# Cross attention's last unit: all score steps ahead of most value products, and four value products between the first turns of the probabilities

## Chip, core and metric

The kernel runs on one core of a Trainium2 chip. The metric is the device time of one execution in microseconds (us), lower is better. A core has a matrix engine (PE, with its weight loads, PEld), a vector engine (DVE), a scalar engine (ACT), GpSimd (POOL) and SyncE (SP), which here only starts DMA transfers. Each engine runs its own instructions strictly in the order in which they are written and waits at semaphores for the others, so an instruction that waits holds up everything behind it on its engine.

## The reference

Three blocks follow one another on x of 8 x 64 tokens of width 512, all in float32: cross attention over a context of 8 x 1601 tokens, a differential attention between the heads of each token with a feed forward, and a mixture of 32 experts (6 per token). The change touches the end of the first:

```
def cross_attention(x_q, x_k, x_v):            # x_k = x_v = context, B=8, L=64, S=1601
    Q = (x_q @ W_Q + b_Q)  -> (B, 16 heads, L, 32)
    K = (x_k @ W_K + b_K)  -> (B, 16, S, 32)
    V = (x_v @ W_V + b_V)  -> (B, 16, S, 32)
    attn = softmax(Q @ K^T / sqrt(32))
    return (attn @ V) @ W_O + b_O
x = x + cross_attention(layernorm(x), ctx, ctx)
x = x + differential_attention_and_ffn(layernorm(x))   # per token: 32 x 32 products of heads, softmax, then att2 @ v
x = x + mixture_of_experts(layernorm(x))
```

## The kernel before

**Units.** `queries_and_cross_attention` runs 16 units (b, h): a batch b of 8 and a half h of the heads (8 heads, 256 columns of K and V). In each unit PE makes the values of its half for the 1601 context tokens as seven value products (`values(b, h, v)`, v = 0 to 6, two tiles of 128 tokens each, the last one tile of 65 rows; 24 matmuls, the last 12), and eight score steps (`scores(b, h, i)`, two groups g of heads by four chunks n of 402 tokens). Value product v goes to a bank of PSUM, the matrix engine's result memory, given by `V_BANK`; ACT casts it to the high part (L596) and DVE subtracts that to get the low part (L741). A score step fills two banks of 0 to 3 and DVE copies both to `prob`, taking the row maxima on the way (L754). When a group's four steps are kept, ACT takes its exponentials in place (`exponentials`, two of each group, L602).

**Turns.** Then come 14 turns (g, t), numbered n = 7g + t: `turn` transposes two tiles of the probabilities into bank 6 or 7 (L471), ACT casts them to the high part (L615), DVE forms the low part (L771), and `weigh` multiplies them with the values (L484) one turn later. After the seven turns of a group DVE adds the halves (L779), PE selects (L494), DVE scales and writes `oT` (`output`, L791). In every unit but the last the key products of the next unit (`keys`) stand between the turns; the last unit, (7, 1), has no next one, so nothing stands there.

**The order in the last unit before.** PE: v0, steps 0 and 1, v1, select, v2, steps 2 and 3, v3, v4, steps 4 and 5, v5, steps 6 and 7, v6, then the turns (`STEPS_BEHIND`). ACT: the casts of v0 to v6, with the exponentials of the second block's heads (`head_exponentials`, L656) behind v2 and the unit's own two behind v3 and v4. DVE follows the same order and carries in its gaps the work of one tile (128 tokens, number t = 2) of the second block: row maximum behind v0 (L845), its subtraction behind v1 (L852), `row_sum` behind v3 (L857 to L861), and the eight sums `reduce` 16 to 23 (L831), of which 16 and 17 stood behind v5 and v6 and the others behind turns 1, 2, 4, 6, 8 and 9.

**POOL.** It waits for `row_sum`, makes three small weights (L319 to L324), then eight products `attended(t, i)` (L334) into two buffers in turn: product i waits until DVE has summed product i - 2, and DVE's `reduce` 16 + i waits for product i. Behind the eighth sum POOL squares (L340), DVE takes the mean square (L865), ACT the root (L629), DVE the reciprocal (L872), POOL scales (L344).

**SP.** Behind the last value product (`v_full`) it loads rows, x, two tiles' data and the weight slabs 1 and 2 over the memory of the context and its weights, which are free then; behind the eighth sum (`red_done`, since POOL's two buffers are slab 0's memory, `x_tok`) it loads slab 0 (W_O) and six others. All engines meet at the end of the block; the second block (`last_head_and_feed_forward`) begins with POOL's bias on `oT` (L1158) and PE's product of `oT` with slab 0 (L1483).

Of the kernel before, what the change touches and what calls it, by code (L numbers as in the profile page):

```python
# [21 lines left out]
B, L, D = 8, 64, 512  # L22
# [13 lines left out]
NV = -(-ST // 2)  # L36
# [34 lines left out]
def queries_and_cross_attention(nc, a, keep):  # L71
# [6 lines left out]
    with ExitStack() as ctx:  # L78
# [106 lines left out]
        freed_by = (2, 4, 5, NV)  # L185

        @block.sync
        def _(sp):
# [91 lines left out]
            for s in (1, 2):  # L280
                sp.dma_start(keep["slabs"][s], a["slabs"][s]).then_inc(keep["w_loaded"][s], 16)
            sp.wait_ge(red_done, 24 * (TT - 1))
            for s in (0, 4, 3, 5, 6, 7, 8):
                place = slab[:].rearrange("p (k n) -> p k n", k=KD) if s == 0 else keep["slabs"][s]
                sp.dma_start(place, a["slabs"][s]).then_inc(keep["w_loaded"][s], 16)
# [95 lines left out]
        def _(pe):  # L381
# [20 lines left out]
            def values(b, h, v):  # L402

                if (b, h, v) == (0, 0, 0):
                    pe.wait_ge(wkv_lo_done, 2)
                    pe.wait_ge(q_lo_done, KD)
                if v < 2:
                    pe.wait_ge(pT_lo_done, b * 28 + (14 * h + 13 + v))
                elif v < 5:
                    pe.wait_ge(v_lo_done, b * 14 + (7 * h + v - 1))  # L410
                else:
                    pe.wait_ge(o_done, b * 4 + (2 * h + v - 4))
                f = slice(D + 256 * h, D + 256 * h + 256)
                for st in tiles(v):
                    r = rows(st)
                    for k in range(KD):
                        s = slice(P * st, P * st + r)
                        ins = mm3(nc, ps[0:r, V_BANK[v], 256 * (st % 2):256 * (st % 2) + 256], c_hi[:, k, s],
                                  c_lo[:, k, s], wkv_hi[:, k, f], wkv_lo[:, k, f], k == 0, k == KD - 1)
                ins.then_inc(v_full, 1)  # L420
# [38 lines left out]
            def turn(b, h, g, t):  # L459
                n = 7 * g + t  # L460
                if n < 2:
                    pe.wait_ge(v_lo_done, b * 14 + (7 * h + 5 - n))
                else:
                    pe.wait_ge(pT_lo_done, b * 28 + (14 * h + 14 + n - 1))
# [9 lines left out]
            def weigh(b, h, g, t):  # L474
                n = 7 * g + t
                pe.wait_ge(pT_lo_done, b * 28 + (14 * h + 14 + n + 1))
                if t == 0:
                    pe.wait_ge(v_lo_done, b * 14 + (7 * h + 6 + g))
# [45 lines left out]
            def unit(b, h, last):  # L524
# [3 lines left out]
                for v in range(NV):  # L528
                    values(b, h, v)
                    for i in STEPS_BEHIND[v]:  # L530
                        scores(b, h, i)
                    if v == 1 and (b or h):
                        select(*((b, 0) if h else (b - 1, 1)), 1)
                for g in range(2):
                    for t in range(NV):
                        turn(b, h, g, t)
                        if t == 2:
                            sums(b, h, g)
# [47 lines left out]
        def _(act):  # L586
# [6 lines left out]
            def values(b, h, v):  # L593
# [3 lines left out]
                               ps[0:r, V_BANK[v], 0:256 * w].rearrange("p (a c) -> p a c", c=64)).then_inc(v_hi_done, 1)  # L597
# [60 lines left out]
            def unit(b, h, last):  # L658
# [7 lines left out]
                for v in range(NV):  # L666
# [8 lines left out]
                for g in range(2):  # L675
                    for t in range(NV):
                        turned(b, h, g, t)
                        if (g, t) in ((0, 1), (0, 3)):
                            exponentials(b, h, 2 + t // 2)
# [51 lines left out]
        def _(dve):  # L731
# [6 lines left out]
            def values(b, h, v):  # L738
# [3 lines left out]
                                        ps[0:r, V_BANK[v], 0:256 * w].rearrange("p (a c) -> p a c", c=64),  # L742
# [131 lines left out]
            def behind_values(b, h, v):  # L874
# [17 lines left out]
                if b == B - 1 and v > 4:  # L892
                    reduce(t, 11 + v)

            def behind_turn(b, h, g, s):
# [24 lines left out]
                else:  # L920
                    if n in (1, 2, 4, 6, 8, 9):
                        reduce(t, 18 + (1, 2, 4, 6, 8, 9).index(n))
# [17 lines left out]
            def unit(b, h, last):  # L940
# [5 lines left out]
                for v in range(NV):  # L946
# [11 lines left out]
                for g in range(2):  # L958
                    for t in range(NV):
                        turned(b, h, g, t)  # L960
                        for half in () if last else HALVES_AT[7 * g + t]:
# [1317 lines left out]
```

## Time and profile before

| | |
|---|---|
| three runs | 1458.3, 1454.91, 1457.27 us, median 1457.27 |
| profiled execution | 1456.9 us, its span 1455.0 us (1.9 us lie outside the span) |
| granted PE clock, mean of the span | 0.988 |
| busy over the span | PE 96%, PEld 82%, DVE 64%, ACT 43%, POOL 42% |
| the last unit on PE | from 934.2 to 986 us; DVE's last output of it ends at 987.3 us |
| its value and score part | to 959.2 us, PE busy throughout |
| its 14 turns | 959.2 to 987.3 us, PE with gaps |

Times of the trace are us from the span's start. In a timeline a row gives start, duration, engine, line of the kernel, operation, output <- input, shapes and count; where the engine was idle before, how long and who released it stands in brackets. Matmuls are pipelined: how long PE is occupied is read from start to start.

### The profile page before, as it was taken

What the parts mean: (1) busy time and instruction counts of PE and PEld (TensorE: products, weight loads), DVE (VectorE), ACT (ScalarE), POOL (GpSimd) and SP (SyncE); (2) the same over time, 40 slices, a digit from 0 to 9 for tenths busy, and PEclk for the clock granted to TensorE, in tenths of its full rate; (3) what the DMA queues carried; (4) which work ended last, traced back from release to release, by engine and by line L of the source; (5) the groups of instructions that cost most, each with busy time, mean ns of one, the idle gap of its engine ahead of it and who ended that gap; (6) DMA issues with size and microseconds to landing.
All of it is one profiled execution on the core that took longest, in us unless ns stands there. A gap on an engine that the chain in (4) does not pass through costs nothing. (4 is left out here: it accounts for less than half of the span.)

```text
span 1455.0 us, 23749 instructions
## 1 busy us (share of the span) xinstructions
PE 1404.1 (96%) x8920; PEld 1191.6 (82%) x8920; DVE 926.0 (64%) x1991; ACT 624.5 (43%) x1065; POOL 607.5 (42%) x276
## 2 busy tenths in 40 slices
PE   6999999999999999999999999988899999999998
PEld 5999999999899998999998989973677646766664
DVE  6545555554388664459675547884942277988885
ACT  4345354354443534535335443452222124666663
POOL 5007007004464920737570246455840025566662
PEclk9999999999999999999999999999999899999999
DMA  5103004013001112300301310037000468999997
GB/s 208 70 2 95 1 5 132 1 41 122 32 5 46 57 33 73 118 7 5 103 2 69 105 56 2 1 136 306 1 1 1 155 242 298 364 365 371 366 370 212
DMA packets 62052, 166.50 MB, mean 114 GB/s; under 512 B 14851, under 2 KB 31747, under 8 KB 52870
## 3 DMA queue, kind: packets, MB, share of 16 engines
q1 hardware_dynamic: 52550, 143.17, 26.7%
q0 software_dynamic: 9408, 22.03, 6.1%
q8 instruction: 65, 1.06, 0.3%
q14 instruction: 29, 0.24, 0.1%
HBM read 145.77 MB, written 19.40 MB: 114 GB/s over the span
## 5 line engine op out<-in xcount | busy, mean ns | idle before, releaser
L66 PE MATMUL ps_x<-wkv_hi,c_hi 128*128 128x256 f32 (+1 forms) x832 | 241.2, 290 | 0.0
L68 PE MATMUL ps_x<-wkv_hi,c_lo 128*128 128x256 f32 (+1 forms) x832 | 234.2, 281 | 0.0
L67 PE MATMUL ps_x<-wkv_lo,c_hi 128*128 128x256 f32 (+1 forms) x832 | 234.2, 281 | 0.0
L293 POOL TENSOR_TENSOR c_hi<-c_raw,ones 128x1608 fp32r<-128x1608 f32 x30 | 88.2, 2940 | 323.5 <-DMA c_raw<-ctxT 323.5
L771 DVE TENSOR_TENSOR pT<-ps_x,pT 128x512 fp32r<-128x512 f32 (+1 forms) x224 | 145.1, 648 | 118.0 <-ACT pT L615 115.3
L66 PE MATMUL ps_x<-c_hi,wkv_hi 128*128 128x402 f32 x512 | 195.9, 383 | 13.7 <-DVE c_lo L977 12.4
L615 ACT CAST pT<-ps_x 128x512 fp32r<-128x512 f32 (+1 forms) x224 | 124.5, 556 | 160.7 <-PE ps_x L471 157.6
L596 ACT CAST vv<-ps_x 128x512 fp32r<-128x512 f32 (+1 forms) x112 | 62.1, 555 | 278.4 <-PE ps_x L68 278.4
L67 PE MATMUL ps_x<-c_lo,wkv_hi 128*128 128x402 f32 x512 | 178.0, 348 | 0.0
L68 PE MATMUL ps_x<-c_hi,wkv_lo 128*128 128x402 f32 x512 | 178.0, 348 | 0.0
L66 PEld LDWEIGHTS ps_x<-wkv_hi,c_hi 128*128 128x128 f32 (+1 forms) x832 | 153.5, 184 | 17.0 <-issue 17.0
L741 DVE TENSOR_TENSOR vv<-ps_x,vv 128x512 fp32r<-128x512 f32 (+1 forms) x112 | 72.9, 651 | 139.1 <-ACT vv L596 139.1
L312 POOL TENSOR_TENSOR x_tok<-t_q,t_k 128x1024 f32<-128x1024 f32 x48 | 114.2, 2398 | 98.7 <-PE ps_x L521 56.6
L68 PEld LDWEIGHTS ps_x<-wkv_hi,c_lo 128*128 128x128 f32 (+1 forms) x832 | 153.6, 185 | 0.0
L67 PEld LDWEIGHTS ps_x<-wkv_lo,c_hi 128*128 128x128 f32 (+1 forms) x832 | 153.2, 184 | 0.0
L484 PE MATMUL ps_x<-pT,vv 128*128 128x256 f32 (+1 forms) x832 | 138.7, 288 | 9.3 <-DVE pT L771 9.0
L735 DVE SCALAR_TENSOR_TENSOR kT_lo<-ps_x,bk,kT_hi 128x402 fp32r<-128x402 f32 x128 | 81.1, 634 | 94.1 <-ACT kT_hi L590 93.7
L484 PEld LDWEIGHTS ps_x<-pT,vv 128*128 128x128 f32 (+1 forms) x832 | 125.4, 189 | 15.4 <-DVE pT L771 13.7
L754 DVE TENSOR_SCALAR_CACHE_REDUCE prob<-ps_x 128x402 f32<-128x402 f32 (+1 forms) x256 | 131.1, 569 | 0.0
L471 PE MATMUL ps_x<-ident,prob 128*128 128x128 f32 (+1 forms) x832 | 127.7, 273 | 0.0
L296 POOL TENSOR_TENSOR c_lo<-c_raw,c_hi 128x1608 fp32r<-128x1608 f32 x31 | 113.4, 3659 | 19.0 <-ACT c_hi L709 16.6
L1722 POOL DMA_INDIRECT acc<-e_mix,e_row_out x40 | 90.1, 2254 | 69.1 <-ACT e_mix L1993 27.1
(329 smaller groups left out, 2908.4 us busy)
## 6 DMA issues: line engine op xcount, KB each, us to landing
e_gu_raw<-w_gu SPq DMA_DIRECT2D x43, 1024.0 KB, 17.8
c_raw<-ctxT SPq DMA_DIRECT2D x32, 804.0 KB, 5.0
e_w_dn<-w_dn SPq DMA_DIRECT2D x42, 512.0 KB, 16.5
x_tok<-slabs SPq DMA_DIRECT2D x13, 1024.0 KB, 4.8
spare<-slabs SPq DMA_DIRECT2D x8, 1024.0 KB, 11.8
h_late<-slabs SPq DMA_DIRECT2D x4, 1024.0 KB, 16.7
e_mix<-shared SPq DMA_DIRECT2D x2, 1536.0 KB, 9.4
wkv_raw<-w_qkv SPq DMA_DIRECT2D x2, 1024.0 KB, 8.9
```

Source lines behind the costliest of these rows:

```text
L66: nc.tensor.matmul(out, a_hi, b_hi, start=start, stop=False)
L67: nc.tensor.matmul(out, a_hi, b_lo, start=False, stop=False)
L68: return nc.tensor.matmul(out, a_lo, b_hi, start=False, stop=stop)
L293: nc.gpsimd.tensor_tensor(c_hi[:, :, chunk(c)], c_raw[:, :, chunk(c)], ones[:, 0:1].unsqueeze(2).to_broadcast([P, KD, CW]), ALU.mult).then ...
L296: nc.gpsimd.tensor_tensor(c_lo[:, :, chunk(c)], c_raw[:, :, chunk(c)], f32(c_hi[:, :, chunk(c)]), ALU.subtract).then_inc(split_done, 1)
L312: nc.gpsimd.tensor_tensor(slab[:, 2 * D * (i % 2):2 * D * (i % 2) + 2 * D].rearrange("p (a b d) -> p a b d", a=2, b=2 * H2), q[:, 2 * i:2 ...
L471: ins = nc.tensor.transpose(ps[0:r, 6 + n % 2, c:c + P], prob[:, 2 * g + j, P * st:P * st + r], ident[:])
L484: ins = nc.tensor.matmul(ps[:, 4 + g, 256 * j:256 * j + 256], vv[0:r, st, 2 * g + j].rearrange("p l c -> p (l c)"), pT[0:r, n % 2, st % 2, ...
L615: nc.scalar.copy(pT[0:r, n % 2, 0:w, :, 0].rearrange("p a j c -> p (a j) c"), ps[0:r, 6 + n % 2, 0:256 * w].rearrange("p (a c) -> p a c", ...
L754: ins = nc.vector.tensor_scalar(prob[:, p, CW * n:CW * n + w], ps[:, 2 * (i % 2) + j, 0:w], 0.0, None, ALU.add, ALU.max, accum_out=pmax[:, ...
L771: nc.vector.tensor_tensor(pT[0:r, n % 2, 0:w, :, 1].rearrange("p a j c -> p (a j) c"), ps[0:r, 6 + n % 2, 0:256 * w].rearrange("p (a c) -> ...
L1722: nc.gpsimd.indirect_dma_start(out=a[f"acc{r % 2}"], out_offset=bass.IndirectOffsetOnAxis(ap=row_out[:, r % U:r % U + 1], axis=0), in_=y[: ...
```

## The change

It touches the last unit alone, but for one order on SP. PE: v0, steps 0 to 3, v1, select, steps 4 and 5, v2, steps 6 and 7, and then v3, v4, v5, v6 behind the turns 0, 1, 2, 3, each ahead of that turn's `weigh`. The four late value products use banks 0, 1, 2 and 0 of the scores. ACT: both exponentials of the first group behind v1 and v2, `head_exponentials` behind the second of them, casts of v3 to v6 behind those of turns 0 to 3. DVE: the same order; `row_sum` stands behind the low part of v3, which is behind turn 0's, and the eight sums stand behind turns 2 to 9, one each. SP: slab 4 moves ahead of slabs 1 and 2.

```diff
+        END = (B - 1, 1)
+        END_ORDER = [("v", 0), ("s", 0), ("s", 1), ("s", 2), ("s", 3), ("v", 1), ("s", 4), ("s", 5), ("v", 2), ("s", 6), ("s", 7)]
+        END_VALUE = {0: 3, 1: 4, 2: 5, 3: 6}
+        END_BANK = [6, 7, 6, 0, 1, 2, 0]
+        def value_bank(b, h, v):
+            return END_BANK[v] if (b, h) == END else V_BANK[v]
...
@@ sync
-            for s in (1, 2):
+            for s in (4, 1, 2):
                 sp.dma_start(keep["slabs"][s], a["slabs"][s]).then_inc(keep["w_loaded"][s], 16)
             sp.wait_ge(red_done, 24 * (TT - 1))
-            for s in (0, 4, 3, 5, 6, 7, 8):
+            for s in (0, 3, 5, 6, 7, 8):
...
@@ tensor, values
+                elif (b, h) == END and v > 2:
+                    pe.wait_ge(sc_kept, b * 16 + (8 * h + (7 if v < 5 else 8)))
+                    if v == 6:
+                        pe.wait_ge(v_lo_done, b * 14 + (7 * h + 4))
...
@@ tensor, turn
-                    pe.wait_ge(v_lo_done, b * 14 + (7 * h + 5 - n))
+                    pe.wait_ge(v_lo_done, b * 14 + (7 * h + (5 if (b, h) != END else 3) - n))
@@ tensor, weigh
-                if t == 0:
+                if (b, h) == END and g == 0:
+                    pe.wait_ge(v_lo_done, b * 14 + (7 * h + t + 1))
+                if (b, h) == END and t == 0:
+                    pe.wait_ge(o_done, b * 4 + (2 * h + 1 + g))
+                elif t == 0:
@@ tensor, unit
-                for v in range(NV):
+                for kind, n in END_ORDER if last else ():
+                    if kind == "v":
+                        values(b, h, n)
+                    else:
+                        scores(b, h, n)
+                    if (kind, n) == ("v", 1):
+                        select(b, 0, 1)
+                for v in () if last else range(NV):
...
                         turn(b, h, g, t)
+                        if last and g == 0 and t in END_VALUE:
+                            values(b, h, END_VALUE[t])
@@ scalar, unit
-                for v in range(NV):
+                if last:
+                    values(b, h, 0)
+                    values(b, h, 1)
+                    exponentials(b, h, 0)
+                    values(b, h, 2)
+                    exponentials(b, h, 1)
+                    head_exponentials(old)
+                for v in () if last else range(NV):
...
                         turned(b, h, g, t)
+                        if last and g == 0 and t in END_VALUE:
+                            values(b, h, END_VALUE[t])
@@ vector, behind_values
-                if b == B - 1 and v > 4:
-                    reduce(t, 11 + v)
@@ vector, behind_turn
-                    if n in (1, 2, 4, 6, 8, 9):
-                        reduce(t, 18 + (1, 2, 4, 6, 8, 9).index(n))
+                    if 2 <= n <= 9:
+                        reduce(t, 14 + n)
@@ vector, unit
-                for v in range(NV):
+                for kind, n in END_ORDER if last else ():
+                    if kind == "s":
+                        scores(b, h, n)
+                        continue
+                    values(b, h, n)
+                    if n == 1:
+                        output(*before, 1)
+                    behind_values(b, h, n)
+                for v in () if last else range(NV):
...
                         turned(b, h, g, t)
+                        if last and g == 0 and t in END_VALUE:
+                            values(b, h, END_VALUE[t])
+                            if t == 0:
+                                behind_values(b, h, 3)
```

## Rows read from the trace of the kernel before

**Rows 1.** Busy time by stretch: start:end, length, engines, granted clock, DMA share, GB/s.

```profile
959.20:963.30 4.10, 1.04 (x11) 0.81 (x9) 3.99 (x13) 1.58 (x5) 3.15 (x3) 1.00 0.65 174
963.30:967.20 3.90, 3.90 (x21) 3.90 (x21) 3.05 (x4) 2.63 (x5) 3.14 (x2) 0.56 0.90 313
983.50:987.40 3.90, 1.95 (x10) 1.35 (x10) 2.15 (x7) 0.30 (x2) 1.05 (x1) 1.00 1.01 420
```

**Rows 2.** Waits from 934 to 988 us: who for whom, total, times, longest.

```profile
PE ps_x L484 <- DVE pT L771: 8.2, 7, 3.1
POOL x_tok L334 <- DVE t_k L831: 3.6, 3, 1.9
```

**Rows 3.** PE's timeline, value products and score steps (start, duration, line, operation).

```profile
941.46 0.61 PE L494 MATMUL ps_x<-both,sel 128*128 128x128 f32 x4
941.82 0.36 PE L66 MATMUL ps_x<-wkv_hi,c_hi 128*128 128x256 f32 x1
...
944.86 0.45 PE L66 MATMUL ps_x<-kT_hi,qbd 64*128 64x402 f32 x2
...
946.16 0.39 PE L66 MATMUL ps_x<-wkv_hi,c_hi 128*128 128x256 f32 x1
...
959.19 1.03 PE L471 MATMUL ps_x<-ident,prob 128*128 128x128 f32 x8
963.28 1.01 PE L484 MATMUL ps_x<-pT,vv 128*128 128x256 f32 x4 [3.06 <-DVE pT L771]
```

**Rows 4.** DVE's timeline, copies of two score steps and the end of `row_sum`.

```profile
939.61 0.57 DVE L754 TENSOR_SCALAR_CACHE_REDUCE prob<-ps_x 128x402 f32<-128x402 f32 x1
...
940.60 0.57 DVE L754 TENSOR_SCALAR_CACHE_REDUCE prob<-ps_x 128x402 f32<-128x402 f32 x1
...
952.21 0.23 DVE L861 TENSOR_SCALAR t_rlam<-t_rinv,t_lam 128x16 f32<-128x16 f32 x1
```

**Rows 5.** ACT's timeline, the cast of v3 and the end of the exponential behind it.

```profile
949.35 0.59 ACT L596 CAST vv<-ps_x 128x512 fp32r<-128x512 f32 x1 [2.83 <-PE ps_x L68]
...
951.36 0.19 ACT L602 ACTIVATION_READ_ACCUMULATOR prob<-prob,nmax 128x1 f32 x1
```

**Rows 6.** POOL's timeline, weights and products.

```profile
952.52 0.62 POOL L319 TENSOR_TENSOR x_tok<-t_att,t_rinv 128x256 f32<-128x256 f32 x1 [27.11 <-DVE t_rlam L861]
...
954.62 7.07 POOL L334 TENSOR_TENSOR x_tok<-t_att,t_v 128x1024 f32<-128x1024 f32 x3
```

**Rows 7.** DVE's timeline, the last sum and what follows it.

```profile
978.35 1.21 DVE L831 TENSOR_REDUCE t_k<-x_tok 128x64 f32<-128x1024 f32 x1
979.48 0.68 DVE L771 TENSOR_TENSOR pT<-ps_x,pT 128x512 fp32r<-128x512 f32 x1
...
986.41 0.92 DVE L791 TENSOR_TENSOR oT<-ps_x,rsb 32x64 f32<-32x64 f32 x4 [0.87 <-PE ps_x L494]
```

**Rows 8.** PE's timeline further on, two gaps of middle length.

```profile
1002.53 5.85 PE L1437 MATMUL ps_h<-spare,t_att 128*128 128x512 f32 x13 [1.59 <-ACT t_att L1229]
...
1147.26 2.21 PE L2082 MATMUL ps_e<-ident,xm 128*128 128x128 f32 x12 [1.94 <-PEq L1516]
```

**Rows 9.** Busy time by stretch around these two gaps (columns as in rows 1).

```profile
1000.00:1005.00 5.00, 3.40 (x12) 1.65 (x11) 2.18 (x5) 1.50 (x4) 0.00 (x0) 1.00 1.02 414
...
1149.00:1151.00 2.00, 1.58 (x7) 0.78 (x5) 1.22 (x2) 0.70 (x2) 0.45 (x1) 0.50 0.74 289
```

**Rows 10.** SP's DMA issues, and PE's first row of the next block.

```profile
959.38 1.29 SPq L274 DMA_DIRECT2D spare<-rows  x3
...
979.59 0.33 SPq L285 DMA_DIRECT2D x_tok<-slabs  x1
...
989.75 5.93 PE L1483 MATMUL ps_h<-x_tok,oT 128*128 128x512 f32 x8 [3.44 <-POOL oT L1158]
```

**Rows 11.** DMA issues from 958 to 980 us: count, KB each, landing time.

```profile
spare<-slabs SPq DMA_DIRECT2D x3, 1024.0 KB, 10.6
x_tok<-slabs SPq DMA_DIRECT2D x1, 1024.0 KB, 4.8
```

More of the change, by code:

```diff
@@ L417, in values @@
                         s = slice(P * st, P * st + r)
-                        ins = mm3(nc, ps[0:r, V_BANK[v], 256 * (st % 2):256 * (st % 2) + 256], c_hi[:, k, s],
+                        ins = mm3(nc, ps[0:r, value_bank(b, h, v), 256 * (st % 2):256 * (st % 2) + 256], c_hi[:, k, s],
                                   c_lo[:, k, s], wkv_hi[:, k, f], wkv_lo[:, k, f], k == 0, k == KD - 1)
@@ L596, in values @@
                 nc.scalar.copy(vv[0:r, 2 * v:2 * v + w, :, 0].rearrange("p a j c -> p (a j) c"),
-                               ps[0:r, V_BANK[v], 0:256 * w].rearrange("p (a c) -> p a c", c=64)).then_inc(v_hi_done, 1)
+                               ps[0:r, value_bank(b, h, v), 0:256 * w].rearrange("p (a c) -> p a c", c=64)).then_inc(v_hi_done, 1)
             def exponentials(b, h, p):
@@ L741, in values @@
                 nc.vector.tensor_tensor(vv[0:r, 2 * v:2 * v + w, :, 1].rearrange("p a j c -> p (a j) c"),
-                                        ps[0:r, V_BANK[v], 0:256 * w].rearrange("p (a c) -> p a c", c=64),
+                                        ps[0:r, value_bank(b, h, v), 0:256 * w].rearrange("p (a c) -> p a c", c=64),
                                         f32(vv[0:r, 2 * v:2 * v + w, :, 0].rearrange("p a j c -> p (a j) c")),
```

## The prediction

> **What bounds the kernel now.** I read four views, in this order. The busy time by stretch first: PE works through the value and score part of the last unit without a pause, then is busy for 1.04 of the first 4.1 us of the turns and about half of the last 3.9 us [rows 1]. The waits say for what: PE's `weigh` waits 8.2 us in all for DVE's low parts of the turned probabilities, 3.06 us of it at the first turn [rows 2, 3]. That is what the change aims at. The timelines of DVE and POOL tell more. Beside the turns runs another chain, of one tile of the second block: `row_sum` on DVE ends at 952.44 us, POOL makes weights and eight products, DVE sums each [rows 4, 6]. Here POOL waits 3.6 us for DVE and DVE never for POOL, so this chain has room [rows 2]. DVE goes from its last sum straight into the tenth turn's low part at 979.48 and ends the unit at 987.33 [rows 7]: behind 975 us it is DVE, not PE, that sets the pace. DVE runs in order, so whatever makes its sums late makes the turns behind them late. All engines meet behind the unit and the next block starts with a product of `oT`, so the unit's end passes on at full size.
>
> **The change, step by step.** No work is added or removed. Everything is moved, and I follow the chain that I expect to end last.
>
> *Scores first.* Up to v0 nothing changes, and DVE begins its copies of step 0 at 939.61 as before. Two copies of a step take 0.99 us (939.61 to 940.60) [rows 4], a step on PE 0.65 us (two from 944.86 to 946.16) [rows 3]. Steps 0 and 1 end on PE at 938.5. Step 2 needs step 0's banks, free at about 940.7, and step 3 those of step 1, free at 941.7. Before, v1 stood in this place and hid the copies; now PE waits some 2.1 us and then 0.3 us more, and ends step 3 at 942.4. Queued behind this wait are v1, select, steps 4 and 5, and v2: with 3.04 us for a value product (941.82 to 944.86), 0.36 us for select and 1.30 us for two steps [rows 3] that is 942.4 + 3.0 + 0.4 + 1.3 + 3.0 = 950.1 for the end of v2.
>
> *The start of the other chain.* ACT's cast of v2 starts 0.1 us later, at 950.2, and the exponential behind it ends 2.2 us after the cast's start (949.35 to 951.55) [rows 5], at 952.4. Turn 0 waits for it; 0.4 us of transposes and v3 bring PE to 955.9, and v3's cast starts at 956.0. DVE's `row_sum` now stands behind the low part of v3. Before, it ended 3.09 us after that cast's start (949.35 to 952.44) [rows 4, 5]; so it now ends at about 959.05, **6.6 us later**.
>
> *POOL's chain.* Weights take 2.10 us (952.52 to 954.62), a product 2.36 us (7.07 / 3) [rows 6]. If POOL never waits, the last product ends 0.08 + 2.10 + 8 x 2.36 = 21.05 us behind `row_sum`, at 980.1, and DVE's last sum, 1.13 us (978.35 to 979.48) [rows 7], ends at 981.3. Does it never wait? Products 2 to 7 need the sums 0 to 5. Walking DVE's order with the durations above, sum 0 comes behind turn 2 and v5's low part at about 964.5 and sum 1 at 966.7, both before POOL has ended product 1 or 2, and each later sum ends 0.5 to 1 us before POOL asks for it. So POOL runs through, and DVE waits for it instead, some 0.5 us at three or four of the sums. Before, the last sum ended at 979.48; it moves by +6.6 for the start and by -4.8 for the waits and pauses that vanish (27.0 us from `row_sum` to the end of the last sum before, 22.2 us now): **+1.8 us**. Without any wait for POOL, DVE's own queue, which got `row_sum` and two sums more behind turn 0, would be about as early as before, so there is no gain even then.
>
> *The tail.* From the last sum to the unit's end it is 7.85 us (979.48 to 987.33) [rows 7]; two short waits of DVE for ACT go, since PE and ACT run ahead: -0.2 us. Sum so far: **+1.6 us**, unit's end at 988.9.
>
> *PE's clock.* Before, the granted clock fell to the half level (1.2 GHz) behind the gap of 3.06 us: 0.56 over the 3.9 us from 963.3 [rows 1, 3]. That gap closes, which gives nothing, as PE is not what ends last there. The new gap of 2.1 us at 938.6 is ahead of a stretch in which PE does set the pace. The trace has gaps on both sides of it: behind one of 1.59 us the clock stayed full, behind one of 1.94 us it was half [rows 8, 9]. The bounds of the cost are 0 and about 1.9 us (half of 3.9 us at the half level). The nearer row is the one that fell, but a part of a half-clock stretch would lie on time in which PE waits for DVE's copies anyway, and the gap need not meet the fall in each execution; I take **+1.0 us**. In turns 4 to 13 PE's gaps grow to 1.5 to 2.0 us; before, half-busy stretches kept the full clock [rows 1]. A fall there is hidden by POOL's 2.36 us a turn but for the last weighs and select: 0 to 0.8 us, of which I take nothing.
>
> *SP and the loads.* The last value product ends at 965.8 (four of them, turns, weighs and sums in PE's order) and not at 959.2, so the loads that started at 959.38 start 6.6 us later, with slab 4 ahead of slabs 1 and 2. The next block needs `x1_in` and `on_in` behind 988 us; they stay over 10 us ahead. With 10.6 us to landing for the slabs [rows 11] the old set was in by 973.3; with one slab more, some 2.5 us, the new one is in by about 982. Slab 0 is asked for when the sums end, at 981.4, instead of 979.59 [rows 10], and lands 4.8 us later, or about 5.5 us behind that bit of queue: 987. PE needs it at 989.75 + 1.6 = 991.3. So the cost is nothing, under a cover of 4 us; the seven slabs behind it have one fewer to carry, and no wait of PE for them is there to be won. ACT's and DVE's casts of v3 to v6 change place, not number; `head_exponentials` ends at 953.4 and delays turn 0's cast to 953.4, hidden under v3.
>
> Sum: 1.6 + 1.0 = +2.6 us. The profiled execution of 1456.9 us (span 1455.0 and 1.9 outside) becomes 1459.5, the median of 1457.27, which lies 0.4 above it, **1459.9 us**.
>
> **The rivals.**
>
> *The gaps are filled and PE's order sets the end (faster).* For it: PE waits 8.2 us at the weighs [rows 2], and 10.5 us of value products (3.0 x 3 and half of one) go among them. Less 3.1 us of new waits (2.1, 0.3, and 0.7 for the exponential ahead of turn 0) this gives -5 us: 1452.2 us. Against it: DVE and POOL as above. The Trainium skill, Perfetto Trace Analysis, Optimization Strategies (DMA part), has the general goal of keeping the Matmul engine as high-utilised as possible, which speaks for the change; its next sentence, to look for the engine that blocks, speaks for this sum.
>
> *The half clock falls on the way to v2 (slower).* Place: v1 and v2, from 941 us. Price: up to 1.9 us on top of 1.6, with up to 0.8 at the end of the unit: +3.5 to +4.3, 1460.8 to 1461.6 us. It decides from a loss of 1.3 us. For it speaks the gap of 1.94 us that ended at the half level; against it the one of 1.59 us that did not [rows 8, 9].
>
> *POOL's chain isn't the later one.* If `row_sum` comes out 1.8 us earlier than I walk it, DVE's own queue ends the unit as before: about -0.2 us, 1457.1 us.
>
> *The loads are late (slower).* If the later set takes 5 us more than before, slab 0 lands behind the bias and the next block waits for it: 1461 us or more. The room of 4 us speaks against it.
>
> **How the numbers follow.** About 0.2% (2.9 us) is what a measurement of this kernel can tell from no change. Chances: the forecast, with a clock loss below 1.3 us, 0.48; the half clock in full 0.38; gaps filled 0.06; POOL's chain not the later 0.05; loads late 0.03. So faster 0.06, same 0.53, slower 0.41. The forecast's own range is 1458.5 to 1460.2. The whole range takes in the unchanged time and the dearest clock case with the scatter of the runs: 1455.9 to 1462.4.
>
> **What would show it.** Right: DVE's `row_sum` near 959, POOL's eight products without a pause (19 us in one piece), DVE waiting for POOL at L831, the last sum near 981.3, the last `output` ending near 989 to 991; a gap of 2 us on PE near 939 and a clock below 1.00 behind it. Wrong: `row_sum` before 957, POOL waiting for DVE as before, the turns' end before 986, or PE waiting for slab 0 behind POOL's bias.

## The result and the profile after

The changed kernel takes 1459.51 us (median of 16 runs, 1457.5 to 1461.17) against 1457.57 us for the kernel before on the same chips; the ratio is 1.0016, 95% interval 1.0008 to 1.0023, or 1.2 to 3.4 us more. One of the 16 runs of the kernel before, at 2556 us, was in a slower state and is not in the ratio. The profiled execution has a span of 1459.1 us against 1455.0.

| mark, us | before | after | moved |
|---|---|---|---|
| start of the last unit's v0 on PE | 934.2 | 934.1 | -0.1 |
| end of `row_sum` | 952.44 | 960.43 | +8.0 |
| start of the low part behind the last sum (L771, now L804) | 979.48 | 982.38 | +2.9 |
| start of the unit's last `output` (L791, now L824) | 986.41 | 989.69 | +3.3 |
| start of the next block's product of `oT` on PE (L1483, now L1526) | 989.75 | 993.02 | +3.3 |
| start of the third block's first PE row (L2082, now L2125) | 1147.26 | 1151.19 | +3.9 |

The delay arises in the last unit and is carried to the end; 0.7 us more come from the first product of the next block, which takes 6.46 us from start to start instead of 5.77, at the half clock level for longer. That part differs from execution to execution, and the median moved by less than this one trace.

The waits between 934 and 990 us of the changed kernel (who <- for whom, total, times, longest). They answer to [rows 2]:

```profile
PE ps_x L499 <- DVE pT L804: 6.1, 7, 1.7
PE ps_x L66 <- DVE prob L787: 2.4, 2, 2.2
DVE t_k L864 <- POOL x_tok L341: 1.4, 3, 0.5
```

PE's waits at the weighs fell from 8.2 to 6.1 us only, 2.4 us of a new kind came, and where POOL waited 3.6 us for DVE, DVE now waits for POOL. PE's timeline at the new wait, and the busy time of that stretch (columns as in [rows 1]), to be held against the gap of [rows 3]:

```profile
940.65 0.53 PE L66 MATMUL ps_x<-kT_hi,qbd 64*128 64x402 f32 x2 [2.19 <-DVE prob L787]
```

```profile
940.00:945.00 5.00, 4.34 (x24) 3.55 (x25) 3.90 (x17) 0.00 (x0) 0.00 (x0) 0.66 0.00 0
945.00:950.00 5.00, 5.00 (x45) 4.62 (x44) 2.58 (x7) 2.21 (x3) 0.00 (x0) 1.00 0.02 5
```

The clock fell to the half level behind the gap. POOL's timeline, which answers to [rows 6]:

```profile
960.52 0.62 POOL L326 TENSOR_TENSOR x_tok<-t_att,t_rinv 128x256 f32<-128x256 f32 x1 [35.19 <-DVE t_rlam L894]
...
962.62 18.59 POOL L341 TENSOR_TENSOR x_tok<-t_att,t_v 128x1024 f32<-128x1024 f32 x8
```

POOL starts 8.0 us later and runs its eight products in one piece. DVE's timeline, the first, three later and the last of its sums, and the two rows that answer to [rows 7]:

```profile
965.65 1.21 DVE L864 TENSOR_REDUCE t_k<-x_tok 128x64 f32<-128x1024 f32 x1
...
974.32 1.22 DVE L864 TENSOR_REDUCE t_k<-x_tok 128x64 f32<-128x1024 f32 x1 [0.42 <-POOL x_tok L341]
...
976.61 1.22 DVE L864 TENSOR_REDUCE t_k<-x_tok 128x64 f32<-128x1024 f32 x1 [0.48 <-POOL x_tok L341]
...
981.25 1.22 DVE L864 TENSOR_REDUCE t_k<-x_tok 128x64 f32<-128x1024 f32 x1 [0.49 <-POOL x_tok L341]
982.38 1.28 DVE L804 TENSOR_TENSOR pT<-ps_x,pT 128x512 fp32r<-128x512 f32 x2
...
989.69 0.92 DVE L824 TENSOR_TENSOR oT<-ps_x,rsb 32x64 f32<-32x64 f32 x4 [1.25 <-PE ps_x L509]
```

PE's last `select`, for which that last output waits, before and after:

```profile
985.60 0.71 PE L494 MATMUL ps_x<-both,sel 128*128 128x128 f32 x4 [0.78 <-DVE both L779]
```

```profile
988.50 1.08 PE L509 MATMUL ps_x<-both,sel 128*128 128x128 f32 x4 [0.78 <-DVE both L812]
```

The granted clock over this `select` was 1.00 before and 0.58 after, and DVE's wait for it grew from 0.87 to 1.25 us.

SP's issues, which answer to [rows 10]:

```profile
967.19 1.28 SPq L281 DMA_DIRECT2D spare<-rows  x3
...
982.49 0.33 SPq L292 DMA_DIRECT2D x_tok<-slabs  x1
```

Slab 0 landed 5.5 us behind its issue, at 988.0, and PE needed it at 993.0.

### The profile page after: what moved, and what is told of

The parts are those of the page before. It is cut to its first block and busy times, and to the rows that moved or that the text cites. A ratio compares the mean times of both kernels' runs of the same rounds, so it can differ in the third digit from the quotient of the medians.

```text
span 1459.1 us, 23755 instructions
## 1 busy us (share of the span) xinstructions
PE 1404.4 (96%) x8920; PEld 1191.6 (82%) x8920; DVE 926.9 (64%) x1991; ACT 623.7 (43%) x1065; POOL 607.1 (42%) x276
## 5 line engine op out<-in xcount | busy, mean ns | idle before, releaser
L804 DVE TENSOR_TENSOR pT<-ps_x,pT 128x512 fp32r<-128x512 f32 (+1 forms) x224 | 145.1, 648 | 117.0 <-ACT pT L639 114.4
```

The source lines that it names most:

```text
L804: nc.vector.tensor_tensor(pT[0:r, n % 2, 0:w, :, 1].rearrange("p a j c -> p (a j) c"), ps[0:r, 6 + n % 2, 0:256 * w].rearrange("p (a c) -> ...
```

## The experiments

All are read by the same marks: the end of `row_sum`, the start of the last sum, the start of the last output. The ratios are to the kernel before, each from 6 to 16 runs of the kernel, so they carry about 0.1% either way; the marks, from one trace each, carry the finer reading. In kernels marked * the unit began later or earlier than in the kernel before by what stands in brackets, which is to be taken off. The last output starts behind PE's last `select`, and DVE's wait for it was 0.87 us in some executions and up to 1.39 in others, depending on the clock (at a granted clock of 1.00 PE takes 0.71 us for it, at 0.50 1.22 us); the fifth column has it, since differences of half a microsecond in the last output can be this alone.

| kernel | `row_sum` ends | last sum starts | last output starts | its wait for the last `select` | ratio, 95% interval |
|---|---|---|---|---|---|
| before | 952.44 | 978.35 | 986.41 | 0.87 | 1 |
| after | 960.43 | 981.25 | 989.69 | 1.25 | 1.0016 (1.0008 to 1.0023) |
| e1_fill | 959.35 | 980.21 | 988.80 | 1.39 | 1.0012 (1.0001 to 1.0022) |
| e2_rowsum * (+0.3) | 958.28 | 981.75 | 989.83 | 0.87 | 1.0016 (1.0006 to 1.0027) |
| e3_pool | 960.84 | 979.93 | 988.81 | 1.39 | 1.0006 (0.9996 to 1.0016) |
| e4_nofill | 960.63 | 984.70 | 992.77 | 0.87 | 1.0037 (1.0023 to 1.0050) |
| e5_order | 959.09 | 979.94 | 988.01 | 0.87 | 0.9997 (0.9985 to 1.0009) |
| e6_sums | 958.88 | 980.06 | 990.07 | 1.38 | 1.0018 (1.0006 to 1.0030) |
| e7_both * (-0.4) | 953.67 | 975.66 | 985.68 | 1.39 | 0.9990 (0.9978 to 1.0001) |
| e8_late | 962.85 | 983.53 | 992.11 | 1.39 | 1.0042 (1.0027 to 1.0056) |
| e9_both_fill * (-0.3) | 953.80 | 975.82 | 985.47 | 0.87 | 0.9992 (0.9981 to 1.0002) |
| e10_fill2 | 959.41 | 980.25 | 988.84 | 1.39 | 1.0015 (1.0005 to 1.0026) |
| e11_slabs | 961.71 | 982.55 | 990.63 | 0.87 | 1.0039 (1.0025 to 1.0053) |
| e12_split * (-0.2) | 951.72 | 976.83 | 986.85 | 1.38 | 0.9996 (0.9987 to 1.0006) |

My theory had three parts: the product chain on POOL and DVE, started late by `row_sum`, sets the unit's end; the half clock behind the new gap adds about 1 us; the value products between the turns bring nothing to the end, as PE isn't what ends last. The rivals were PE's own order, DVE's own queue, and the loads.

### e1_fill: PE kept busy in the new gap

```diff
+                    if (kind, n) == ("s", 1):
+                        pe.wait_ge(pT_lo_done, b * 28 + (14 * h + 14))
+                        for k in range(18):
+                            nc.tensor.matmul(ps[:, 7, 0:256], c_hi[:, k % KD, 0:P], wkv_hi[:, k % KD, D:D + 256], start=True, stop=True)
```

> The changed kernel, with 18 matmuls of 256 columns into the free bank 7 behind score step 1 of the last unit, so that PE does not stand idle while DVE copies steps 0 and 1. They lie in time in which PE waited 2.19 us, and change no result. Theory of the clock: the granted clock stays 1.00 between 940 and 945 (it was 0.66), v1's cast starts near 945.6 instead of 946.7, row_sum ends near 959.2 instead of 960.4, the unit's last output ends near 989.4 instead of 990.6: 1.2 us less than the changed kernel, ratio to before about 1.0008. Rival (the new wait for the copies alone costs, the clock doesn't matter): v1 and all behind it stay where they are, unit's end 990.6, ratio 1.0016.

The busy time of the stretch and DVE's timeline of e1_fill:

```profile
940.00:945.00 5.00, 4.88 (x40) 4.16 (x40) 3.80 (x17) 0.00 (x0) 0.00 (x0) 1.00 0.01 3
```

```profile
959.12 0.23 DVE L899 TENSOR_SCALAR t_rlam<-t_rinv,t_lam 128x16 f32<-128x16 f32 x1
...
980.21 1.22 DVE L869 TENSOR_REDUCE t_k<-x_tok 128x64 f32<-128x1024 f32 x1 [0.48 <-POOL x_tok L342]
...
988.80 0.92 DVE L829 TENSOR_TENSOR oT<-ps_x,rsb 32x64 f32<-32x64 f32 x4 [1.39 <-PE ps_x L510]
```

The clock stayed full, `row_sum` and the last sum came 1.1 and 1.0 us earlier, the last output 0.9 us. The unit's last output was expected 1.2 us earlier; 0.14 of what is missing is the slower last `select`. The clock theory holds, with 1.1 us for the fall in this pair of traces. The ratio alone (1.0012 against 1.0016) couldn't have told it.

### e2_rowsum and e6_sums: the chain's start

e2_rowsum:

```diff
+                            if t == 0:
+                                behind_values(b, h, 3)
                             values(b, h, END_VALUE[t])
-                            if t == 0:
-                                behind_values(b, h, 3)
```

> The changed kernel with row_sum on DVE ahead of v3's low part instead of behind it, in a gap of 2.1 us in which DVE waits for ACT's cast of v3. Theory of the product chain (row_sum's end sets POOL's eight products, these set DVE's last sum, this the unit's end): row_sum ends near 957.8 instead of 960.4; POOL starts 2.6 us earlier, DVE's waits for POOL (1.4 us) vanish and its own queue takes over, so that the unit's end moves by 1.4 to 2.6 us, to 988.0 to 989.2; ratio to before 1.0002 to 1.0008. Rival (PE's late value products and turns set the pace): unit's end stays at 990.6, ratio 1.0016.

`row_sum` came 2.4 us earlier with the unit's start taken off, as expected, and the end gained only 0.2 us: the last sum started no earlier (981.75, or 981.45 with the start taken off, against 981.25), though 0.4 us of that is a fall of the clock at the gap that took more than in the changed kernel. POOL's timeline of e2_rowsum says why:

```profile
960.47 4.76 POOL L342 TENSOR_TENSOR x_tok<-t_att,t_v 128x1024 f32<-128x1024 f32 x2
967.54 4.70 POOL L342 TENSOR_TENSOR x_tok<-t_att,t_v 128x1024 f32<-128x1024 f32 x2 [2.31 <-DVE t_k L865]
```

With two buffers POOL's third product waits for the first sum, and that stands behind turn 2 and v5's low part on DVE. So my expectation missed: in the changed kernel two things start the chain nearly together, `row_sum` and the place of the first sum (POOL's second product ended at 967.3, the first sum at 966.8). Moving one leaves the other. e6_sums makes the edit of e2_rowsum and moves the sums as well:

```diff
-                    if 2 <= n <= 9:
-                        reduce(t, 14 + n)
+                    if 1 <= n <= 8:
+                        reduce(t, 15 + n)
```

> The changed kernel with row_sum ahead of v3's low part, as in e2_rowsum, and the eight sums behind turns 1 to 8 instead of 2 to 9. In e2_rowsum POOL waited 2.31 us for the first sum, so the theory is now that the place of the first sum in DVE's order sets the chain, together with row_sum: the first sum starts near 963 instead of 966, POOL's products run in one piece from 960.5 to 979, the last sum ends near 980.4 behind turn 8 and turn 10's low part starts 1.3 us earlier than in the changed kernel, the last output near 988.5 instead of 989.7: ratio 1.0006 to 1.0010. Rival (PE's turns or DVE's total work set the pace from turn 4 on): no change to e2_rowsum, 1.0016.

The last sum started at 980.06 and now stands a turn earlier, as expected, yet the last output started at 990.07, not 988.5. In this execution the half level lay longer over v1 and again over the late turns (busy time by stretch of e6_sums):

```profile
940.00:945.00 5.00, 4.37 (x21) 3.75 (x22) 3.81 (x17) 0.00 (x0) 0.00 (x0) 0.53 0.00 0
945.00:950.00 5.00, 5.00 (x36) 4.62 (x35) 1.38 (x5) 2.04 (x3) 0.00 (x0) 0.78 0.02 5
...
975.00:980.00 5.00, 4.35 (x19) 3.96 (x19) 4.16 (x6) 1.76 (x3) 5.00 (x3) 0.50 1.06 426
```

Held against the changed kernel's trace, e6_sums shows nothing. But e11_slabs, which up to here is the changed kernel and differs only in SP's loads, had the same fall: 0.53 and 0.79 in the first two stretches and 0.50 in the third. DVE's last rows of e6_sums and e11_slabs:

```profile
990.07 0.92 DVE L825 TENSOR_TENSOR oT<-ps_x,rsb 32x64 f32<-32x64 f32 x4 [1.38 <-PE ps_x L510]
```

```profile
990.63 0.92 DVE L825 TENSOR_TENSOR oT<-ps_x,rsb 32x64 f32<-32x64 f32 x4 [0.87 <-PE ps_x L510]
```

Against it, `row_sum` ends 2.8 us earlier in e6_sums and the last sum starts 2.5 us earlier. The last output starts 0.6 us earlier, or 1.1 with the longer wait for `select` taken off, where 1.2 was expected. So moving both starts does gain about a microsecond; the rest of the 2.5 us is one more turn behind the last sum, in which DVE waits for ACT. Both figures come from one pair of traces, and the ratio (1.0018) doesn't show the gain.

### e3_pool: POOL's products made short

```diff
+                if t == TT - 2 and i > 1:
+                    nc.gpsimd.tensor_tensor(slab[:, 2 * D * (i % 2):2 * D * (i % 2) + D].rearrange("p (a d h) -> p a d h", a=1, d=2 * D2),
+                                            att2[:, 2 * i:2 * i + 1].unsqueeze(2).to_broadcast([P, 1, 2 * D2, H2]),
+                                            v[:].unsqueeze(1).to_broadcast([P, 1, 2 * D2, H2]), ALU.mult).then_inc(prod_done, 1)
+                    return
```

> The changed kernel with half of the multiplication left out in the last six of POOL's eight products of the tile beside the last unit (half the elements each, some 1.2 us instead of 2.33), so that the output is not the reference's. All the rest stands. Theory of the product chain: DVE no longer waits for POOL (1.4 us in three waits), the last sum ends 1.4 us earlier or a little more, unit's end near 989.2, ratio to before about 1.0006. Beyond that nothing is gained, since DVE's own queue follows at once. Rival (POOL is beside the point): unit's end 990.6, ratio 1.0016.

DVE's timeline of e3_pool:

```profile
979.93 1.21 DVE L870 TENSOR_REDUCE t_k<-x_tok 128x64 f32<-128x1024 f32 x1
...
988.81 0.92 DVE L830 TENSOR_TENSOR oT<-ps_x,rsb 32x64 f32<-32x64 f32 x4 [1.39 <-PE ps_x L515]
```

DVE's waits for POOL are gone, the last sum starts 1.3 us earlier and the last output 0.9 us. `row_sum` ended 0.4 us later here than in the changed kernel, behind a longer stretch at the half clock, and the last `select` took 0.14 us more, so POOL's products cost the changed kernel 0.9 to 1.4 us, and no more: DVE's own queue of turns, low parts and sums is nearly as late. That is the second half of the theory: two engines that feed each other end within a microsecond and a half.

### e4_nofill: scores first without value products between the turns

```diff
-        END_ORDER = [..., ("v", 2), ("s", 6), ("s", 7)]
-        END_VALUE = {0: 3, 1: 4, 2: 5, 3: 6}
+        END_ORDER = [..., ("v", 2), ("s", 6), ("s", 7), ("v", 3), ("v", 4), ("v", 5), ("v", 6)]
+        END_VALUE = {}
...
@@ scalar, unit
                     head_exponentials(old)
+                    for v in range(3, NV):
+                        values(b, h, v)
```

> The changed kernel with v3 to v6 directly behind score step 7 and ahead of turn 0, so that only the scores-first order is kept and nothing stands between the turns. PE: step 7 ends near 953.2, v6 near 963.8, turn 0 near 964.2 instead of 953.8. Theory of the product chain: row_sum ends near 960 as in the changed kernel, POOL's products run from 962 to 981, but DVE's turns start 9 us later, so that its sums (one behind each of turns 2 to 9, 1.8 us a turn) end near 984 instead of 982.4: unit's end 991.5 to 993, ratio 1.002 to 1.003. Rival (the four value products between the turns are what is gained, as many us as PE waited for): unit's end 6 us or more later than 990.6, ratio 1.005 or above.

DVE's timeline of e4_nofill:

```profile
984.70 1.22 DVE L867 TENSOR_REDUCE t_k<-x_tok 128x64 f32<-128x1024 f32 x1 [0.47 <-POOL x_tok L342]
...
992.77 0.92 DVE L827 TENSOR_TENSOR oT<-ps_x,rsb 32x64 f32<-32x64 f32 x4 [0.87 <-PE ps_x L510]
```

The last output starts 6.4 us later than before the change and 3.1 us later than after it (ratio 1.0037), a little more than I had expected (its end at 991.5 to 993; it was 993.7). This takes the change apart: the scores-first order with its later sums costs 6.4 us at the unit's end (some 1.4 of them by the half clock behind the same gap), and the four value products between the turns give 3.1 us of that back. By the marks the rival's 6 us is out, but "brings nothing" in my theory was too strong: in this order the filling pays, only less than the order costs.

### e5_order: v1 back between the scores

```diff
-        END_ORDER = [("v", 0), ("s", 0), ("s", 1), ("s", 2), ("s", 3), ("v", 1), ("s", 4), ("s", 5), ("v", 2), ("s", 6), ("s", 7)]
+        END_ORDER = [("v", 0), ("s", 0), ("s", 1), ("v", 1), ("s", 2), ("s", 3), ("v", 2), ("s", 4), ("s", 5), ("s", 6), ("s", 7)]
...
+                    values(b, h, 2)
                     exponentials(b, h, 0)
-                    values(b, h, 2)
                     exponentials(b, h, 1)
```

> The changed kernel with v1 back behind score steps 0 and 1, so that it hides DVE's copies: v0, steps 0 and 1, v1, steps 2 and 3, v2, steps 4 to 7, then turn 0; on ACT v2's cast goes ahead of the first exponential. All else as in the changed kernel. Theory (the wait of 2.2 us and the half clock behind it are on the path to the first sum): PE reaches turn 0 near 951 instead of 953.8, row_sum ends near 957.4, the first sum starts near 962.4 instead of 965.65, the last one near 978 instead of 981.25, and the unit's last output starts near 986.4 instead of 989.7, where it was before the change: ratio to before 0.9995 to 1.0000. Rival (DVE's own queue behind turn 0 is the bound, whatever comes first): the last output stays near 989.7, ratio 1.0016.

Right in direction and half in size. The gap of 2.19 us and the half clock behind it are gone, but PE meets the copies again ahead of step 6, and this time the clock falls there (PE's timeline and busy time of e5_order):

```profile
949.22 0.46 PE L67 MATMUL ps_x<-kT_hi,qbd 64*128 64x402 f32 x2 [0.97 <-DVE prob L788]
```

```profile
950.00:955.00 5.00, 4.84 (x30) 4.33 (x29) 3.15 (x13) 2.48 (x4) 0.00 (x0) 0.66 0.00 0
```

`row_sum` ended at 959.09, not 957.4, and the last output started at 988.01: 1.7 us less than the changed kernel and 1.6 us more than before. PE reached turn 0 at 951.47, near the 951 expected, so the miss lies behind it. From step 7 to turn 0 it took 1.26 us and from turn 0 to turn 1 4.33 us; in e7_both, which has the same order on PE and kept the clock at 1.00 there, 0.88 and 3.31. So 1.4 us of the 1.7 us missing are a half clock in another place, and by this estimate e5_order would without it stand within some tenths of the kernel before. The ratio, 0.9997, can't be told from 1; it lies below that of the changed kernel, but their intervals still touch.

### e8_late: the kernel before with the late chain alone

```diff
-                if v == 3:
+                if v == 3 and b < B - 1:
                     row_sum(t)
-                if b == B - 1 and v > 4:
-                    reduce(t, 11 + v)
...
-                    if n in (1, 2, 4, 6, 8, 9):
-                        reduce(t, 18 + (1, 2, 4, 6, 8, 9).index(n))
+                    if n == 0:
+                        row_sum(t)
+                    if 2 <= n <= 9:
+                        reduce(t, 14 + n)
```

> The kernel before, with its own order on PE and ACT, but with row_sum on DVE behind turn 0's low part and the eight sums behind turns 2 to 9, as the change has them. Theory (the delay of the product chain alone makes the unit longer): row_sum ends near 965.1 instead of 952.44, POOL's products run in one piece to 985.8, the last sum ends near 987, 7.5 us later than before, and the last output starts near 993.9: ratio 1.005. Rival (DVE's slack takes it up, or the change's cost is in PE's gap alone): last output near 986.4 to 988, ratio 1.000 to 1.001.

POOL's timeline of e8_late, and DVE's:

```profile
965.02 18.47 POOL L335 TENSOR_TENSOR x_tok<-t_att,t_v 128x1024 f32<-128x1024 f32 x8
```

```profile
962.62 0.23 DVE L862 TENSOR_SCALAR t_rlam<-t_rinv,t_lam 128x16 f32<-128x16 f32 x1
...
983.53 1.22 DVE L832 TENSOR_REDUCE t_k<-x_tok 128x64 f32<-128x1024 f32 x1 [0.49 <-POOL x_tok L335]
...
992.11 0.92 DVE L792 TENSOR_TENSOR oT<-ps_x,rsb 32x64 f32<-32x64 f32 x4 [1.39 <-PE ps_x L495]
```

With PE's and ACT's order untouched and no new gap, moving DVE's `row_sum` and sums alone costs 5.7 us at the unit's end, ratio 1.0042; 5.2 of them stand at the last sum already, the other half microsecond is the slower last `select`. This shows the chain at work by itself. `row_sum` ended 2.2 us earlier than I had worked out, because turn 0's low part, no longer behind a sum, came earlier too. From `row_sum`'s end to the last sum's start it is 20.7 us here, 20.8 in the changed kernel and 20.9 in e1_fill and e5_order: where POOL runs in one piece this length is fixed. Before it was 25.9 us, pauses included. So in these kernels the last sum is later by what `row_sum` is later, less 5.0 to 5.2 us. By this sum, an estimate, `row_sum` could have moved by some 5 us at no cost in this chain; the change moved it by 8.

### e7_both, e9_both_fill and e12_split: towards a faster order

e7_both is e5_order with the sums behind turns 1 to 8, `row_sum` ahead of turn 0 instead of behind v3's low part, and:

```diff
@@ scalar, unit
                     values(b, h, 1)
+                    head_exponentials(old)
                     values(b, h, 2)
...
-                    head_exponentials(old)
@@ vector, unit, behind the loop over END_ORDER
+                if last:
+                    behind_values(b, h, 3)
```

> The order of e5_order, with the exponentials of the second block's heads on ACT between the casts of v1 and v2, row_sum on DVE behind the copies of step 7 and ahead of turn 0, and the sums behind turns 1 to 8. Theory: row_sum ends near 953.7, POOL's products end near 976, DVE's last sum near 976.2, turn 9's low part follows, and the last output starts near 983.5: some 3 us ahead of the kernel before (986.41), ratio 0.998. With this the value products between the turns are worth what PE waited less what DVE needs. Rival (DVE's own work from 954 on is the bound): last output near 986, ratio 1.000.

`row_sum` and the last sum came where they were expected (953.67, 975.66). The end did not: 985.68 instead of 983.5, 0.7 us ahead of before and, with the unit's earlier start taken off, 0.3. Behind the last sum DVE waited 0.35 and 0.85 us for ACT and 0.59 and 1.39 us for PE, and the clock had been at the half level just before (busy time of e7_both):

```profile
970.00:975.00 5.00, 4.48 (x20) 3.77 (x19) 4.16 (x6) 1.18 (x3) 5.00 (x3) 0.50 1.06 417
```

e9_both_fill adds matmuls between the turns:

```diff
+                        if last and 5 <= 7 * g + t <= 11:
+                            pe.wait_ge(v_lo_done, b * 14 + (7 * h + 5))
+                            for k in range(3):
+                                nc.tensor.matmul(ps[:, 1, 0:P], ones[:], ident[:], start=True, stop=True)
```

> The kernel of e7_both with three extra matmuls (ones by the identity, into the free bank 1) behind each of turns 5 to 11, ahead of the weigh that waits for DVE there; they change no result. In e7_both the granted clock was at the half level from 970 to 976 and the last turns waited for ACT and PE (0.35, 0.85, 0.59 and 1.39 us). Theory of the clock in the turns: the clock stays 1.00 from 965 to 983, DVE's waits behind its last sum shrink by 1.2 us or more, the last output starts near 984.5 instead of 985.68 on the same start of the unit: ratio to before 0.998 to 0.9985. Rival (these waits are PE's order, not its clock, or the extra matmuls delay the weighs): last output at 985.7 or later, ratio 0.999 or above.

The clock stayed at 1.00 from 965 to 985, but the last output, expected at 984.5, started at 985.47: it gained 0.2 us, or 0.3 with the starts taken off, which the wait for the last `select` (0.87 instead of 1.39) more than covers. One wait for ACT grew to 1.30 us; that the extra matmuls took the time ahead of the weighs is my reading of it. So the clock in the turns is not shown to cost the tail anything beyond some tenths; what is left is the order of PE, ACT and DVE in the last turns, which no run here changes by itself. e12_split starts from e7_both, moves v3 back between steps 5 and 6, and puts `row_sum` ahead of v3's low part:

```diff
+        END_ORDER = [..., ("v", 2), ("s", 4), ("s", 5), ("v", 3), ("s", 6), ("s", 7)]
+        END_VALUE = {0: 4, 1: 5, 2: 6}
+        END_BANK = [6, 7, 6, 7, 0, 1, 2]
```

> The kernel of e7_both with v3 between score steps 5 and 6 (bank 7, as before the change) and only v4, v5 and v6 behind turns 0 to 2 (banks 0, 1, 2); row_sum on DVE ahead of v3's low part. In e7_both PE still waited 1.3 us for the copies ahead of steps 6 and 7; v3 now hides that. Theory (PE's gaps ahead of turn 0 and the start of the product chain both count): row_sum ends near 952, POOL's products run early, DVE's last sum ends near 976 behind turn 8, and the last output starts near 984.7 instead of 985.68, 1.7 us ahead of the kernel before: ratio 0.9985. Rival (DVE's copies of steps 6 and 7 now hold v4, and DVE's own work is the bound): last output at 985.7 or later, ratio 0.999 to 1.000.

`row_sum` ended at 951.72, even ahead of before, and POOL then waited 4.12 us for the first sum, which now came behind a later turn 0 (POOL's timeline of e12_split):

```profile
962.76 14.01 POOL L342 TENSOR_TENSOR x_tok<-t_att,t_v 128x1024 f32<-128x1024 f32 x6 [4.12 <-DVE t_k L866]
```

It is the lesson of e2_rowsum once more: last output 986.85 instead of 984.7, no gain. e7_both and e9_both_fill have the lowest ratios, 0.9990 and 0.9992, both below that of the changed kernel by intervals that don't meet its own; that either beats the kernel before is not shown, as their intervals reach 1.0001 and 1.0002.

### e10_fill2 and e11_slabs: the clock in the turns, and the loads

e10_fill2 is the changed kernel with both fillings.

> The changed kernel with the 18 matmuls of e1_fill behind score step 1 and the three per turn of e9_both_fill behind turns 5 to 11. Theory: what is left of the change's cost without any half clock in the last unit is the later product chain alone: the last sum starts at 980.2 as in e1_fill, and the last output near 988.2, 1.8 us behind the kernel before (986.41), ratio 1.0008 to 1.0012. Rival (the clock in the turns costs as much as that at the gap): last output near 987.5 or earlier, ratio 1.0005.

The last output started at 988.84, as in e1_fill (988.80). But e1_fill already had the full clock between the turns (1.00 from 965 to 985), so this filling had nothing to save there. What the clock between the turns costs is read better from the changed kernel, which had 0.66 from 970 to 980, against e1_fill: from `row_sum`'s end to the last sum's start it is 20.8 us in the one and 20.9 in the other, so up to the last sum it cost nothing. What remains without the clock's fall at the gap is 2.4 us, of which 0.5 is the last `select`, again at the half level, and 1.9 the chain, near the 1.8 that I gave.

e11_slabs:

```diff
-            for s in (4, 1, 2):
+            for s in (4, 1, 2, 3, 5, 6):
...
-            for s in (0, 3, 5, 6, 7, 8):
+            for s in (0, 7, 8):
```

> The changed kernel with three more weight slabs (3, 5 and 6) asked for ahead of slab 0, so that slab 0 queues behind 3 MB more. Theory of the hidden loads: slab 0 landed at 988.0 in the changed kernel and PE needs it at 993.0, so there are 5 us of cover; 3.1 MB at 0.42 MB per us take 7.5 us, slab 0 lands near 993.5, and the next block's first product starts 0 to 1.5 us later than in the changed kernel: ratio 1.0016 to 1.0026. Rival (the loads are already late in the changed kernel and are its cost): every us counts, 7.5 us more, ratio 1.006 or above.

PE's first row of the next block in e11_slabs:

```profile
995.98 6.53 PE L1527 MATMUL ps_h<-x_tok,oT 128*128 128x512 f32 x8 [5.46 <-DMA x_tok<-slabs]
```

Here a load was late at last: PE waited 5.46 us instead of 3.44, so 2.0 us are slab 0's, somewhat more than the 0 to 1.5 expected (the rest of the way from 1.0016 to 1.0039 has a share of the clock in it: `row_sum` came 1.3 us later than in the changed kernel). 7.5 us of extra transfer cost 2.0 us, so in the changed kernel some 5 us of cover hid the loads. They are no part of its cost.

## Why the prediction was right

The forecast was +2.6 us; the ratio gives +2.3 (1.2 to 3.4), and the time of 1459.51 us lies 0.4 us below the 1459.9 forecast. That closeness is helped by the kernel before, whose median over 16 runs is 0.3 us above the 1457.27 that I started from; the two medians differ by 1.9 us. Point by point, at the marks:

- **PE's new wait**: 2.1 us ahead of the second pair of steps forecast, 2.19 measured: right. The 0.3 us that were to follow at the next step are there in e1_fill (0.46 us from start to start instead of 0.19); in the changed kernel the slower matmuls of the step before cover them.
- **`row_sum`**: 959.05 without the clock's fall; e1_fill, which has none, gives 959.35. Right to 0.3 us.
- **POOL's products**: without a pause, last sum ending 22.2 us behind `row_sum`; 21.95 us (960.43 to 982.38). Right. DVE's waits, 0.5 us at three or four sums: 0.42, 0.48 and 0.49.
- **The last sum**: +1.8 us without the clock: +1.9 in e1_fill (its start 980.21 against 978.35). Right.
- **The tail**: -0.2 us forecast, mis-sized. From the last sum's end to the last output's start it was 6.93 us before (979.48 to 986.41), 7.31 after and 7.45 in e1_fill: +0.4 to +0.5. This is the last `select`: PE took 0.71 us for it at a granted clock of 1.00 before, 1.08 at 0.58 after and 1.22 at 0.50 in e1_fill, and DVE's wait for it grew from 0.87 to 1.25 and 1.39. The prediction had named 0 to 0.8 us for a fall there and taken nothing. Without it the tail is as long as before, so the -0.2 did not come either: of DVE's two waits for ACT one vanished (0.17), the other grew from 0.34 to 0.60.
- **The clock at the gap**: +1.0 us taken between 0 and 1.9. The fall came in all six profiled kernels that have this gap and in neither of the two that fill it. Measured by when the previous head's `output` behind v1 starts (946.83 with the filling): 1.1 us in the changed kernel and 1.4 to 2.4 in the other five. In two of them (e6_sums, e11_slabs) it was 2.4, above the upper bound of 1.9: that bound took a half-clock stretch of 3.9 us, and here the mean clock was 0.53 in the five microseconds from 940 and still 0.78 and 0.79 in the next five. The forecast case was a loss below 1.3 us, and the profiled execution of the changed kernel is the only one of the six that has it: here the forecast was lucky. It should have leaned to the upper bound.
- **The loads**: nothing, with 4 us of cover. They began 7.8 us later, not 6.6 (nearly all of the difference is what the clock took at the gap), and 5 us of cover remained. Right.
- **The rival "the gaps are filled"** is refuted as a sum, but had a true core: e4_nofill shows 3.1 us given back by the value products between the turns, which the forecast did not price by itself.
- **What the prediction did not see**: that POOL's chain had two starts. It checked that the first sums come before POOL asks and found 0.5 to 1 us of room; that room was all there was, so an earlier `row_sum` alone (e2_rowsum, e12_split) is worth nearly nothing.

Added up in the trace, the unit's end moved by +3.3 us: 1.9 at the last sum without the clock (forecast 1.8), 1.0 for the fall at the gap (forecast 1.0) and 0.4 at the last `select` (forecast -0.2 for the tail and nothing for the clock). The mechanism was right, and the tail is the term that was off. The median's +2.3 is nearer to the forecast's +2.6 than the trace is; its interval holds both.

## What to carry to other kernels

Before idle time of an engine is filled, look for the chain that ends last where the filling work comes from and goes to: here the gaps of PE were real, but DVE and POOL, which pass a small side job to each other, ended the unit, and the reordering delayed that job's start by 8 us. Where two engines alternate over two buffers, the place of the first hand-back in the in-order queue counts as much as the start of the job; move both or neither. And work that looks misplaced between two dependent steps may be hiding the drain of a buffer: taken away, it leaves a gap that costs twice, once as a wait and once more as a slower clock.

## What the runs showed of the hardware

- A single wait of PE of 2.19 us behind a busy stretch was followed by the half clock level (1.2 GHz) in six of six profiled kernels, with a granted clock of 0.53 to 0.76 over the five microseconds from 940. The kernel before had kept the full level behind 1.59 us and lost it behind 1.94. But the length of a wait doesn't settle it: behind waits of 0.15, 0.97 and 0.16 us ahead of three steps the clock fell in e5_order (0.66 from 950 to 955) and stayed at 1.00 in e7_both and e9_both_fill, which have the same order on PE there and the same waits within 0.02 us. 18 matmuls of 256 columns, 2.3 us of them, kept it at 1.00 in two of two.
- The price of one such fall differs from kernel to kernel with the same gap, 1.1 to 2.4 us, mostly because the slow stretch differs in length: in the two with 2.4 us the clock averaged 0.53 from 940 to 945 and 0.78 and 0.79 from 945 to 950, in the other four 0.66 to 0.76 and then 0.90 to 1.00. That alone is 0.1% of this kernel, as much as the ratios' own uncertainty. The gain of e6_sums shows only against e11_slabs, an execution with the same fall.
